# GpSimd's readout product with four state rows innermost, and the last piece of the decay table on GpSimd

## The reference, cut to what matters

```python
def step(state, inp):
    qt, kt, vt, bt = inp
    kk = kt[..., :, None] * kt[..., None, :]
    bb = bt[..., None, None]
    state = state * (1.0 - bb * kk) + bb * (vt[..., :, None] * kt[..., None, :])
    out_t = jnp.einsum('bhij,bhj->bhi', state, qt)
    return (state, out_t)
```

## Time and profile before

| | us |
|---|---|
| median of 3 runs | 889.64 (888.16 to 892.07) |
| the profiled execution: span | 888.7 |
| median less that span | 0.9 |
| VectorE busy | 617.1 (69%) |
| GpSimd busy | 452.7 (51%) |
| TensorE busy | 710.7 (80%) |
| ScalarE busy | 355.4 (40%) |

### The profile page before, as it was taken

The page is one execution under the profiler, slowest core; times in us unless marked ns, Lnnn a source line. Parts: engine busy times, 40 slices in busy tenths (PEclk is TensorE's granted clock), DMA queues, the critical chain, the costliest instruction groups (busy, mean ns, idle before and its releaser), DMA issues. The chain is left out here.

```text
span 888.7 us, 20544 instructions
## 1 busy us (share of the span) xinstructions
PE 710.7 (80%) x7708; PEld 478.2 (54%) x7708; DVE 617.1 (69%) x913; ACT 355.4 (40%) x561; POOL 452.7 (51%) x257
## 2 busy tenths in 40 slices
PE   3576759886999999999999999976899689875744
PEld 3354534444677777777777777755676323322221
DVE  3599947888999999999999999963676501100005
ACT  2366635353445545445455544433555211010100
POOL 1588700002999999999999999981111000000000
PEclk9799869998999999999999999987999879979765
DMA  5100000000001010000000000005800679999936
GB/s 109 48 1 0 0 1 0 0 0 14 8 14 38 13 35 12 11 7 12 12 12 12 12 12 8 12 14 198 313 25 1 233 271 412 417 416 416 418 135 213
DMA packets 48891, 86.34 MB, mean 97 GB/s; under 512 B 5232, under 2 KB 32432, under 8 KB 48848
## 3 DMA queue, kind: packets, MB, share of 16 engines
q1 hardware_dynamic: 43248, 81.23, 25.1%
q10 hardware_dynamic: 5600, 4.53, 1.6%
HBM read 76.31 MB, written 9.44 MB: 96 GB/s over the span
## 5 line engine op out<-in xcount | busy, mean ns | idle before, releaser
L898 POOL TENSOR_TENSOR read<-state,q_pos 128x1024 f32<-128x1024 f32 x128 | 300.2, 2365 | 28.5 <-DVE state L1007 22.4
L1007 DVE TENSOR_TENSOR_SCAN state<-fac,ps_up 128x1024 f32<-128x1024 f32 x128 | 290.1, 2278 | 8.6 <-ACT fac L942 8.2
L942 ACT ACTIVATE fac<-ps_xf 128x1016 f32<-128x1016 f32 x128 | 130.2, 1018 | 176.1 <-PE ps_xf L1041 160.2
L1041 PE MATMUL ps_xf<-hot,xtab 64*128 64x128 f32 x2048 | 148.4, 284 | 11.0 <-ACT fac L942 8.9
L1041 PEld LDWEIGHTS ps_xf<-hot,xtab 64*128 64x128 f32 x2048 | 125.4, 188 | 58.0 <-ACT fac L942 43.4
L1041 PE MATMUL ps_up<-hot,utab 64*128 64x128 f32 x2048 | 140.0, 276 | 19.3 <-DVE state L1007 19.3
L1041 PEld LDWEIGHTS ps_up<-hot,utab 64*128 64x128 f32 x2048 | 126.4, 189 | 24.9 <-issue 17.6
L907 POOL TENSOR_TENSOR utab<-tab 128x1024 f32 (+1 forms) x32 | 64.7, 2022 | 94.4 <-SPq L85 94.4
L1086 PE MATMUL ps_o<-read,sel 128*32 128x256 f32 x1024 | 82.4, 393 | 4.0 <-POOL read L898 4.0
L1627 DVE COPY h_t<-ps_ht 128x512 f32<-128x512 f32 x16 | 10.3, 686 | 75.7 <-PE ps_ht L1655 75.7
L997 DVE TENSOR_TENSOR xtab<-tab,ps_k 128x1024 f32<-128x1024 f32 x64 | 59.5, 930 | 1.5 <-PE ps_k L1033 1.5
(11 more groups left out here) (202 smaller groups left out, 995.0 us busy)
## 6 DMA issues: line engine op xcount, KB each, us to landing
w_sb<-in_L_ffn_w SPq DMA_DIRECT2D x32, 2048.0 KB, 19.4
rec_out<-osb SPq DMA_DIRECT2D x128, 32.0 KB, 1.5
ao<-rec_out SPq DMA_DIRECT2D x8, 512.0 KB, 4.4
out_dram<-res ACTq DMA_DIRECT2D x8, 512.0 KB, 2.8
tok<-in_x SPq DMA_DIRECT2D x2, 512.0 KB, 11.2
exp_out<-eo SPq DMA_DIRECT2D x8, 128.0 KB
oq<-exp_out SPq DMA_DIRECT2D x2, 512.0 KB, 3.9
w_nat<-in_L_tok_Wq SPq DMA_DIRECT2D x1, 256.0 KB, 3.1
```

What stands on the lines that cost most here:

```text
L898: nc.gpsimd.tensor_tensor(read[n % 2][:], state[n % 4][:].rearrange("p (b i t) -> p b i t", b=2, i=IB), q_pos[x.s][:, :, x.k].unsqueeze(2) ...
L942: nc.scalar.activation(fac[n % 2][:].rearrange("p (n t) -> p n t", t=T)[:, :, 1:], ps_x[:].rearrange("p (n t) -> p n t", t=T)[:, :, 1:], A ...
L1007: nc.vector.tensor_tensor_scan(state[n % 4][:], fac[n % 2][:], ps_u[n % 2][:], 0.0, ALU.mult, ALU.add)\
L1041: last = nc.tensor.matmul(dst[:, b * 512 + col * T:b * 512 + (col + 1) * T], stationary[rows], pos[rows], start=True, stop=True)
```

## The change

The readout product gets another walk: both the state that it reads and the product that it writes are taken with the four rows i innermost (512 bytes from one to the next), then t, then b, and q is held for four columns in a row. Before, t was innermost: all three went along contiguous columns, and q's 128 columns were gone through anew for each row. The data stay where they were. And piece 2 of the decay table `xtab` passes from VectorE to GpSimd (`late_factors`), which takes k from SBUF where VectorE took it from PSUM. The counts of the semaphores follow.

```diff
-                nc.gpsimd.tensor_tensor(read[n % 2][:], state[n % 4][:].rearrange("p (b i t) -> p b i t", b=2, i=IB),
-                                        q_pos[x.s][:, :, x.k].unsqueeze(2).broadcast_to([P, 2, IB, T]), ALU.mult)\
+                nc.gpsimd.tensor_tensor(read[n % 2][:].rearrange("p b i t -> p b t i"),
+                                        state[n % 4][:].rearrange("p (b i t) -> p b t i", b=2, i=IB),
+                                        q_pos[x.s][:, :, x.k].unsqueeze(3).broadcast_to([P, 2, T, IB]), ALU.mult)\
                     .then_inc(rd_ok, 1)
...
+            def late_factors(i, n):
+                x = Unit(i, n)
+                pool.wait_ge(x_mm, START + x.u - 4)
+                k_feat = tab[:, bass.ds(x.pair, 1), 1, x.k * P:(x.k + 1) * P].rearrange("p o c -> p (o c)")
+                out, feat = table_views(m, xtab, x, 0, 1)
+                cols = slice(D // 2, D)
+                nc.gpsimd.tensor_tensor(out[:, :, :, cols], feat[:, :, :, cols],
+                                        k_feat.rearrange("p (h j) -> p h j", j=D)[:, :, cols].unsqueeze(1)
+                                        .broadcast_to([P, D // 2, HB, D // 2]), ALU.mult).then_inc(t_pool, 1)
+
             def turn(i, last=False):
                 for n in range(2 * UN):
                     readout(i, n)
                     if n % 4 == 1 and not (last and n > 2 * UN - 4):
                         late_updates(i, n + 3)
+                    if n % 4 == 3 and not (last and n > 2 * UN - 4):
+                        late_factors(i, n + 1)
 
             late_updates(0, 0)
+            late_factors(0, 0)
...
-                which, half = ((0, 0), (1, 0), (0, 1))[piece]
                 dve.wait_ge(k_ok, START + x.pair + 1)
...
-                    if n % 4 < 3 and not (last and n >= 2 * UN - 4):
+                    if n % 4 < 2 and not (last and n >= 2 * UN - 4):
                         tables(i, n - n % 4 + 4, n % 4)
...
-                if x.block % 2 == 0:
-                    pe.wait_ge(t_dve, START + 3 * x.v + (3 if x.block else 1))
+                if x.block == 0:
+                    pe.wait_ge(t_dve, START + 2 * x.v + 1)
                 if x.block == 2:
+                    pe.wait_ge(t_pool, START + 2 * x.v + 2)
                     pe.wait_ge(t_act, START + x.v + 1)
```

More of the change, by code:

```diff
@@ L956, in mirror @@
                 x = Unit(i, n)
-                act.wait_ge(t_dve, START + 3 * x.v + 1)
+                act.wait_ge(t_dve, START + 2 * x.v + 1)
                 rows = xtab[x.k][:].rearrange("p i (h j) -> p i h j", j=D)
@@ L990, in tables @@
                 x = Unit(i, n)
-                which, half = ((0, 0), (1, 0), (0, 1))[piece]
                 dve.wait_ge(k_ok, START + x.pair + 1)
[L993 to L1000, removed]
+                dve.wait_ge(u_mm if piece else x_mm, START + x.u - 4)
+                out, feat = table_views(m, utab if piece else xtab, x, piece, 0)
+                nc.vector.tensor_tensor(out, feat, ps_k[:, x.k * P:(x.k + 1) * P].rearrange("p (h j) -> p h j", j=D)
+                                        .unsqueeze(1).broadcast_to([P, D // 2, HB, D]), ALU.mult).then_inc(t_dve, 1)
             def scan(i, n):
@@ L1017, in _ @@
                 ch.link(nc.vector.memset(f[:].rearrange("p (n t) -> p n t", t=T)[:, :, 0], 0.0))
-            for piece in (0, 1, 2):
+            for piece in (0, 1):
                 tables(0, 0, piece)
@@ L1031, in keys @@
                 x = Unit(i, n)
-                pe.wait_ge(t_dve, START + 3 * x.v)
+                pe.wait_ge(t_dve, START + 2 * x.v)
                 nc.tensor.matmul(ps_k[:], ident[:],
@@ L1055, in updates @@
                 if x.block == 0:
-                    pe.wait_ge(t_dve, START + 3 * x.v + 2)
+                    pe.wait_ge(t_dve, START + 2 * x.v + 2)
                 if x.block == 2:
-                    pe.wait_ge(t_pool, START + x.v + 1)
+                    pe.wait_ge(t_pool, START + 2 * x.v + 1)
                 pe.wait_ge(sc_ok, START + x.u - 1)
```

## The result

The changed kernel takes 956.64 us (953.48 to 960.2, 4 runs) where the kernel before takes 889.5: a ratio of 1.0755, 95% interval 1.0723 to 1.0786. It is 67 us slower. The forecast had the direction right, and its whole range (877 to 990 us) holds the result; but it said 917 us, and of the added time it foresaw 27.

The account below looks back on a forecast made before the run. VectorE sets the pace now, with GpSimd half a microsecond a block behind; after the change GpSimd bounds. 10.1 us for longer products plus 17.2 for piece 2 give +27 us, forecast 917 us, range 877 to 990.

Parts of the forecast that it names:

- Part one: Piece 2 leaves VectorE: of 31 pieces of 0.58 us only 16 count, worth 9.3 us.
- Part two: Piece 2 arrives on GpSimd at 1.12 us each: 33.6 us of work, 16.4 filling idle time, so +17.2 us.
- would anything starve GpSimd: GpSimd's queue stays full: chain from piece 2 to the third unit's product 4.5 to 5 us, against 6.6 of work.
- Part three: GpSimd's readout product with the new walk: 2.444 us instead of 2.365, adding 10.1 us over 128 products.
- R: Time of one GpSimd readout product with the new walk, forecast at 2.44 us; break-even at 2.231.
- the case: Scaled case, held likeliest at 0.32: new product takes 2.27 to 2.7 us, kernel 895 to 950 us.
- the prediction's own formula: While GpSimd is the bound, change = 128 x (new product's time - 2.365) + 17.2 us.
- scaled carry-over: GpSimd's strided state step costs 1.98 times 0.355 ns, the ratio from ScalarE's `mirror`; product 2.44 us.
- the added one: ScalarE's extra 0.88 ns a column added whole to GpSimd's product, 904 ns: 3.00 us, kernel 988 us; chance 0.27.
- first rival: The stride is hidden on GpSimd: product 2.09 us, VectorE still sets the pace, 879 us; chance 0.31.
- The signs named in advance: If GpSimd bounds: its idle shrinks to a few us, VectorE's scans wait for `read`, TensorE's `sums` wait for products.
- the second way in which the forecast was to be wrong: GpSimd's queue is full, yet the stage is longer than the sum of its work.

Follow-up runs that it names:

- the four corners: Changed kernel 956.64 us; with old walk 945.72; with piece 2 one product earlier 931.44; with old walk and earlier piece 905.29.
- four buffers: Changed kernel with four `read` buffers instead of two, piece 2 still behind the fourth product: 942.25 us, ratio 1.0586.

## Why the prediction was right in direction and wrong in size

**Part one held.** Piece 2's absence from VectorE is worth half of its time, 9.3 us forecast and 10 measured without any piece, and the wait at a pair's start grew to 1.1 or 1.2 us where 1.18 was worked out.

**Part two held for the work and failed for the waits.** Piece 2 takes 1.15 us on GpSimd, 1.12 forecast. The 17.2 us for work less idle time filled came out as 14.6, where the piece stands early and the walk is the old one. The step that failed is the answer to "would anything starve GpSimd": "TensorE's wait for GpSimd's piece 2 queues `updates` and `sums` behind it, and these have that same slack." I had followed the chain from piece 2 to the third product after it, through a scan, which has 6.6 us. The second product needs no new scan, but it needs a `read` buffer, and the `sums` that free it are the ones queued behind the wait: 3.0 us, against one product of 2.3 to 2.5. Moving the piece one product ahead takes 25.2 us off the changed kernel; in the sum this term stood at nothing. Some 22 us of it are GpSimd's waits in the profile. The prediction also left out that TensorE can run slower behind such a wait: with the old walk its products did so behind 11 of the 31 pieces, GpSimd then waited 2.1 to 2.4 us instead of about 0.7, and the place was worth 41.7 us.

**Part three was mis-sized.** R was forecast at 2.444 us and measured 2.576, inside the case's 2.27 to 2.7; yet the time lies above the case's 895 to 950 us. By the prediction's own formula 2.576 gives 128 x 0.211 + 17.2 = 44 us, or 934; the other 23 us come near what the place was measured at. The walk costs 27.4 us where GpSimd is the bound; the sum had 10.1. Two errors oppose each other: holding q saves 351 ns instead of 273, and the stride costs nearly 0.6 us instead of 0.36. The scaled carry-over from ScalarE's copy was too mild and the added one (0.90) too harsh. That the write is free was right. The Trainium skill (GPSIMD Engine Reference, section 7, "Performance pitfalls for Q7 kernels") warns of strided reads on this engine; the runs agree on the direction. Its one cycle, an estimated 853 ns, is more than the nearly 0.6 us measured here.

Put together: 14.6 for the piece, 27.4 for the walk and 25.2 for the place make the measured loss of 67 us; forecast were 17.2, 10.1 and 0. That they add up proves nothing, since they are differences along one path through the four corners, and another path splits the same loss otherwise (14.6 for the piece, 41.7 for the place, 10.9 for the walk). On either path the place, which the sum had at nothing, is a large term. The direction did not hang on it: with the piece early the kernel is still 42 us slower than before.

**The rivals.** The stride was not hidden; with contiguous operands and the piece early it would have been the first rival's case (879.35 against 879). So close a hit is in part luck: the product took 2.01 us where that rival had 2.09, but with VectorE as the bound this hardly counts. The signs named in advance came half: scans wait for `read` only 3.6 us, since TensorE, not the state buffers, passed GpSimd's lateness on, as waits for `fac`. "GpSimd's queue is full and yet the stage is longer than its sum" was the second way in which the forecast was to be wrong, and it is nearly that: the queue ran empty by half a microsecond in most blocks.

What stays open: of the 11 us between four buffers (942) and the earlier piece (931), some 8 are GpSimd's waits for scans, and which part of these comes from TensorE's lower clock and which from its waits for the piece no run separates.

## What to carry to other kernels

When work moves to an engine that is nearly full, price its place in the queue as well as its length: list for the consumer everything that is queued behind its wait, and follow each of these back to the producer through every buffer count, with the shortest loop first. Here the shortest loop ran through two `read` buffers and was worth about as much as the strided read. And before work is taken off an engine, look at which of its copies stands ahead of a wait that will swallow it.

## What the runs showed of the hardware that was not expected

- On GpSimd, holding one operand for four columns makes a 1024-column product as fast as holding it for 16: 2014 and 2021 ns, against 2365 with both running.
- A 512-byte stride on the read side of that product costs nearly 0.6 us by the means (2576 to 2593 against 2014 ns); on the write side 34 ns (2048 against 2014).
- TensorE's clock fell to 1.2 GHz behind some waits of only 2.0 to 2.2 us, ahead of which it had worked at the full clock; behind other waits, as long or longer, it did not (2.23 us in the changed kernel's block above, and up to 2.82 us in that kernel, where the next 16 products took 1.16 us).
- TensorE's `sums` took 1.09 us for eight products where they read at a 16-byte stride, against 0.64 along contiguous columns.
- When GpSimd's queue is never empty its instructions read longer without coming less often: with the piece early and the old walk a product shows 2449 ns, 84 more than before, while the spacing of products in a row is that of before, 2.32 us. With a mean of 2736 ns, the kernel with the strided read alone has products in a row 2.55 us apart. Here the spacing is the safer reading.
